# Rounded weight quarters transposed by VectorE in 32x32 squares and brought round through memory, instead of by TensorE

## What is computed

```
x = x + S4(x, lengths)            # long convolution over the 1024 positions, masked by a length
x = x + x W1^T + gated low rank   # top 2 of 8 experts, rank 16 each
x = x + x W2^T + low rank         # one of 5 labelers, rank 32
x = x + x w_eff^T                 # W3 rounded to a codebook, below
```

```
lora_delta = lora_B @ lora_A * (LORA_ALPHA / LORA_RANK)
normalized = (weight + lora_delta) / scale
idx = searchsorted(thresholds, normalized, side='left')
w_q = ((cb[idx] - normalized) + normalized) * scale
w_eff = w_q + lora_delta
```

## Time and profile before

| | us |
|---|---|
| three runs, median | 980.62 (980.40 to 981.99) |
| profiled execution | 980.34 |
| its span | 978.5 |
| TensorE busy | 968.8 (99%) |
| VectorE busy | 835.1 (85%) |
| ScalarE busy | 448.2 (46%) |
| GpSimd busy | 276.0 (28%) |
| DMA queue of SyncE, share of 16 engines | 44.2% |

### The profile page before, as it was taken

The page is one execution under the profiler, slowest core; times in us unless marked ns, Lnnn a source line. Parts: engine busy times, 40 slices in busy tenths (PEclk is TensorE's granted clock), DMA queues, the critical chain, the costliest instruction groups (busy, mean ns, idle before and its releaser), DMA issues.

```text
span 978.5 us, 16678 instructions
## 1 busy us (share of the span) xinstructions
PE 968.8 (99%) x4773; PEld 781.7 (80%) x4773; DVE 835.1 (85%) x1663; ACT 448.2 (46%) x855; POOL 276.0 (28%) x346
## 2 busy tenths in 40 slices
PE   9999999999999999999999999999999999999998
PEld 5455459888888788888888888888888888888886
DVE  6899999989954888888988888888889888888863
ACT  3342526253565445545445444455454455454541
POOL 6600100945434332222322223322223322223100
PEclk9999999999999999999999999999999999999999
DMA  8924010102133455555554545655556545555321
GB/s 283 124 46 86 0 44 1 44 1 44 29 68 64 76 109 93 100 98 99 115 103 89 109 90 106 112 95 98 101 96 115 105 87 104 96 104 112 76 44 44
DMA packets 380589, 83.46 MB, mean 85 GB/s; under 512 B 353144, under 2 KB 373432, under 8 KB 380552
## 3 DMA queue, kind: packets, MB, share of 16 engines
q1 hardware_dynamic: 379544, 82.28, 44.2%
q10 hardware_dynamic: 1008, 0.76, 0.3%
HBM read 60.89 MB, written 20.71 MB: 83 GB/s over the span
## 4 chain that ended last, share of the span: by engine, by line
PE 96%; ACT 1%; ACTq 1%; issue 1%; DVE 1%; POOL 0%; DVEq 0%; POOLq 0%
PE bank L816 35%; PE bank L1033 12%; PE bank L971 10%; PE bank L803 7%; PE bank L782 5%; PE bank L837 5%; PE bank L793 4%; PE bank L771 4%; PE bank L807 4%; PE bank L949 3%; PE bank L982 2%; PE bank L843 2%; PE bank L827 1%; PE bank L990 1%; PE bank L915 1%
## 5 line engine op out<-in xcount | busy, mean ns | idle before, releaser
L816 PE MATMUL bank<-Mh,strips_r 128*128 128x512 f32 x1020 | 289.1, 395 | 0.0
L816 PEld LDWEIGHTS bank<-Mh,strips_r 128*128 128x128 f32 x1020 | 189.9, 188 | 40.9
L1109 ACT ACTIVATE SK<-ZZ 64x448 f32<-64x448 f32 x128 | 73.9, 577 | 215.1 <-DVE ZZ L1463 212.7
L577 POOL TENSOR_TENSOR Cl<-QC,Ch 128x256 fp32r<-128x256 f32 x32 | 39.0, 1218 | 450.0 <-ACT Ch L1091 450.0
L816 PE MATMUL bank<-Ml,strips_r 128*128 128x512 f32 x510 | 160.0, 395 | 0.0
L1463 DVE SCALAR_TENSOR_TENSOR ZZ<-ZZ,coef 128x192 f32<-128x192 f32 (+1 forms) x256 | 106.6, 456 | 10.1 <-DVE ZZ L1454 0.2
L816 PEld LDWEIGHTS bank<-Ml,strips_r 128*128 128x128 f32 x510 | 95.9, 188 | 22.6
L971 PE MATMUL bank<-E,A 128*128 128x512 f32 (+1 forms) x320 | 97.8, 466 | 0.0
L1454 DVE SCALAR_TENSOR_TENSOR ZZ<-ZZ,coef 128x384 f32<-128x384 f32 (+1 forms) x128 | 80.0, 625 | 12.8 <-DVE ZZ L1463 6.7
L971 PEld LDWEIGHTS bank<-E,A 128*128 128x128 f32 x320 | 51.0, 191 | 44.9 <-issue 44.3
L803 PE MATMUL bank<-Mh,strips_r 128*128 128x296 f32 x256 | 70.7, 299 | 0.0
(11 more groups left out here) (319 smaller groups left out, 1840.3 us busy)
## 6 DMA issues: line engine op xcount, KB each, us to landing
X<-in_x SPq DMA_DIRECT2D x256, 64.0 KB, 2.3
XT<-in_x SPq DMA_DIRECT2D x256, 64.0 KB, 2.2
out_x<-O SPq DMA_DIRECT2D x62, 256.0 KB, 3.2
toep<-kpad SPq DMA_DIRECT2D x128, 64.0 KB, 2.2
E<-in_L_cond_W SPq DMA_DIRECT2D x8, 512.0 KB, 7.0
vq<-in_L_cond_weight SPq DMA_DIRECT2D x8, 512.0 KB, 3.4
turned<-TB SPq DMA_DIRECT2D x29, 128.0 KB, 2.0
Bt<-turned SPq DMA_DIRECT2D x116, 32.0 KB, 2.1
```

What stands on the lines that cost most here:

```text
L816: pe.matmul(psO[nh][:, :], xs[:, c, :], ms[:, c, nh * BANK:(nh + 1) * BANK], start=(c == 0 and n == 0), stop=False)
L1109: act.activation(SK[ri * N:(ri + 1) * N, hh, :].rearrange("p (c b) -> p c b", b=B), ZZ[hh * N:(hh + 1) * N, :, ri, :], ACT.Copy).then_inc( ...
```

## The change

TensorE's jobs a3, ScalarE's copies of them and GpSimd's diagonal sums go. When VectorE has rounded quarter q, it adds the identity to the two diagonal blocks, and transposes the quarter in squares of 32x32 into dq[q % 2], which is free by then. The SyncE queue writes dq to a new tensor `quarters` in memory so that the squares land in their turned places, and loads A3 from it in one DMA. New waits keep dq (ScalarE's next delta), the comparisons and the tables from overwriting what is not yet stored. Two waits of VectorE (v_ready, quant_init) move from ahead of the branches to behind them. On ScalarE and GpSimd `state_columns` and the first `expand_b` move from behind m(3, 0) to behind m(2, 9).

```diff
-        def stagings(q):
-            return [("a3", q, (q + k) % QUARTERS) for k in range(QUARTERS)]
...
         for mt in range(MT):
-            order += [("lap", mt)] + stagings(0)[mt:mt + 1]
+            order.append(("lap", mt))
...
+                def store_quarter(q):
+                    sp.wait_ge(q_turned, QT_TILES * (q + 1))
+                    for a in range(PARTS):
+                        dst = bass.AP(quarters.tensor, q * P * QCOLS + a * SPAN, [[QCOLS, SPAN], [P, QT_TILES * NC], [SPAN * QCOLS, PARTS], [1, SPAN]])
+                        sp.dma_start(dst, dq[q % 2][a * SPAN:(a + 1) * SPAN, :, :].rearrange("p t k -> p (t k)").rearrange(
+                            "p (n k j) -> p n k j", k=PARTS, j=SPAN)).then_inc(q_stored, 16)
+
+                def load_quarter(q):
+                    sp.wait_ge(q_stored, 16 * PARTS * (q + 1))
+                    sp.dma_start(A3[q % 2][:, :, :], quarters[q].rearrange("p (c o) -> p c o", c=NC)).then_inc(a3_loaded[q], 16)
...
                     elif name == "m":
...
-                            pool.wait_ge(a3_ready, QT_TILES * min(q + 2, QUARTERS))
...
-                        if j == ("m", LAST_Q, 0):
+                        if j == ("m", LAST_Q - 1, MT):
                             pool.wait_ge(cols_ready, 1)
                             expand_b(0, first=True)
...
-                        pe.wait_ge(stage_free, jobno[stagings(q)[-1]] + 1)
-                        pe.wait_ge(a3_ready, QT_TILES * (q + 1))
+                        pe.wait_ge(a3_loaded[q], 16)
...
                         if n == 0 and q >= 2:
                             act.wait_ge(quant_done, q - 1)
+                            act.wait_ge(q_stored, 16 * PARTS * (q - 1))
...
                         if 4 <= mt < 4 + FIXED:
+                            act.wait_ge(q_turned, QT_TILES)
                             compare(2, mt - 4)
...
-                        elif j == ("m", LAST_Q, 0):
+                        elif j == ("m", LAST_Q - 1, MT):
                             state_columns()
...
                     dve.tensor_tensor(vg, vg, inv_g, ALU.mult).then_inc(v_ready, 1)
...
-                    dve.wait_ge(v_ready, q + 1)
-                    dve.wait_ge(quant_init, q + 1)
...
                         with dve.If((n_kept & worth) > 0):
                             first = (n_kept >> (bit + 1)) << (bit + 1)
+                            dve.wait_ge(v_ready, q + 1)
+                            dve.wait_ge(quant_init, q + 1)
...
                     dve.tensor_tensor(qf, qf, df, ALU.add).then_inc(quant_done, 1)
+                    dve.wait_ge(quant_done, q + 1)
+                    for t in range(QT_TILES):
+                        d = qq[q][:, t, (q * QT_TILES + t) * P:(q * QT_TILES + t + 1) * P]
+                        step(dve.tensor_tensor(d, d, ident[:, :], ALU.add))
+                        dve.transpose(df.rearrange("p (c t k j) -> p t c k j", c=NC, k=PARTS, j=SPAN)[:, t],
+                                      qq[q][:, t, :].rearrange("p (c k r) -> p c k r", c=NC, k=PARTS)).then_inc(q_turned, 1)
...
-                dve.wait_ge(stage_full, jobno[stagings(1)[-1]] + 1)
+                dve.wait_ge(q_turned, QT_TILES * TURNED)
...
+                dve.wait_ge(q_stored, 16 * PARTS * TURNED)
                 angles(0)
```

More of the change, by code:

```diff
@@ L66, in resid_stack_kernel @@
     kpad = nc.dram_tensor("kpad", [H, 2, KP], F32, kind="Internal").ap()
+    QUARTERS = 4
+    TURNED = QUARTERS
+    quarters = nc.dram_tensor("quarters", [TURNED, P, 2 * L], F32, kind="Internal").ap()
     turned = nc.dram_tensor("turned", [P, HB * P], F32, kind="Internal").ap()
@@ L78, in place @@
         return t
-    QUARTERS = 4
     QO = L // QUARTERS
@@ L274, in resid_stack_kernel @@
         v_ready, above_done, w2_turned, nat_decay = sem("v_ready"), sem("above_done"), sem("w2_turned"), sem("nat_decay")
-        qt_full, qt_free, a3_ready = sem("qt_full"), sem("qt_free"), sem("a3_ready")
+        qt_full, qt_free = sem("qt_full"), sem("qt_free")
+        q_turned, q_stored, a3_loaded = sem("q_turned"), sem("q_stored"), [sem(f"a3_loaded{q}") for q in range(TURNED)]
         m_full, m_taken, m_lo, lowrank_hi, lowrank_lo = sem("m_full"), sem("m_taken"), sem("m_lo"), sem("lowrank_hi"), sem("lowrank_lo")
@@ L318, in resid_stack_kernel @@
                 order += [("m", q, mt)]
-                if q + 1 < QUARTERS and mt in (2, 4, 6, 7):
-                    order.append(stagings(q + 1)[(2, 4, 6, 7).index(mt)])
         jobs = [j for j in order if j[0] not in ("b3t", "qt0", "qt", "m")]
@@ L492, in _ @@
                 next_w2(7)
-                for q in range(2, QUARTERS):
-                    next_w3(q)
-                sp.wait_ge(stage_full, jobno[stagings(2)[-1]] + 1)
+                def store_quarter(q):
[7 more added lines that the diff above has]
+                    sp.dma_start(A3[q % 2][:, :, :], quarters[q].rearrange("p (c o) -> p c o", c=NC)).then_inc(a3_loaded[q], 16)
+                store_quarter(0)
+                next_w3(2)
+                store_quarter(1)
+                sp.wait_ge(quant_done, 2)
+                load_quarter(0)
+                sp.wait_ge(lowrank_lo, 3)
+                load_quarter(1)
+                next_w3(3)
+                store_quarter(2)
+                sp.wait_ge(m_full, mno["m", 0, MT] + 1)
+                load_quarter(2)
                 load_x(0, X, x_loaded)
                 load_x(0, XT, xt_loaded)
+                store_quarter(3)
+                sp.wait_ge(m_full, mno["m", 1, MT] + 1)
+                load_quarter(3)
                 for half in range(2):
@@ L697, in _ @@
                         pool.tensor_tensor(BLl[:, :], LAp[:, NC, :], BLh[:, :].bitcast(F32), ALU.subtract).then_inc(lowrank_lo, 1)
-                    elif name == "a3" and which[0] == which[1]:
-                        q = which[0]
-                        pool.wait_ge(stage_free, jobno[j] + 1)
-                        for t in range(QT_TILES):
-                            d = A3[q % 2][:, q * QT_TILES + t, t * P:(t + 1) * P]
-                            pool.tensor_tensor(d, d, ident[:, :], ALU.add).then_inc(a3_ready, 1)
                     elif name == "m":
@@ L984, in lap @@
                         start=(it == 0), stop=(it == NC - 1)))
-                def a3(q, n):
-                    if n == q:
-                        pe.wait_ge(quant_done, q + 1)
-                    several(("a3", q, n), 2 * QT_TILES, lambda ps, m: pe.transpose(
-                        ps[:, m * P:(m + 1) * P], qq[q][:, m % QT_TILES, (2 * n + m // QT_TILES) * P:(2 * n + m // QT_TILES + 1) * P], ident[:, :]))
                 def kern():
@@ L1034, in m @@
                     last.then_inc(m_full, 1)
-                do = dict(scale=scale_t, delta=delta, w2t=w2t, codesT=codes_t, codes=codes, nat4=nat4_t, wrt=wrt, qt0=qt0, qt=qt, lap=lap,
-                          a3=a3, m=m)
+                do = dict(scale=scale_t, delta=delta, w2t=w2t, codesT=codes_t, codes=codes, nat4=nat4_t, wrt=wrt, qt0=qt0, qt=qt, lap=lap, m=m)
                 for j in order:
@@ L1324, in _ @@
                             act.activation(BLh[:, :], LAp[:, NC, :], ACT.Copy).then_inc(lowrank_hi, 1)
-                    elif name == "a3":
-                        q, n = which
-                        if (q, n) == (0, 0):
-                            act.wait_ge(quant_done, 2)
-                        take(j, A3[q % 2][:, 2 * n:2 * n + 2, :], stage(j)[:, :].rearrange("p (t o) -> p t o", t=2))
                     else:
```

## The result

| us | before | after |
|---|---|---|
| median of the runs | 981.2 (980.40 to 981.99) | 994.99 (993.45 to 995.89) |
| ratio, 95% interval | | 1.0145 (1.0133 to 1.0157) |
| profiled execution | 980.34 | 995.89 |
| its span | 978.5 | 994.1 |

The changed kernel is slower by 1.45%: 13.8 us between the medians, 15.6 between the two profiled spans. The prediction was 990 in a range of 982 to 1001.

What follows compares the result with a forecast made beforehand. TensorE was taken as the bound before, the table chain after: angles 12.6 us late less 4.0 slack gives 8.6, plus 1.0 for the clock on 980.3 makes 989.9, called 990; range 982 to 1001.

Steps and rivals of the forecast that it cites:

- Bound and slack: Before the tiles: TensorE bounds the kernel; the table chain leading back to its state transpose has 4.0 us of slack.
- What goes from TensorE: Between laps and products m: 64 transposes in 16 groups go, 7.9 us, which become idle time and no gain.
- The laps' stall: TensorE before lap(0): 7.7 us idle until quarter 1 is stored, not on the path that ends last.
- The turn on VectorE: VectorE after rounding each quarter: two diagonal sums and two transposes cost 3.1 us, between 2.7 and 3.2.
- The moved waits: VectorE's rounding loop: branches run beside the product ahead of them, hiding the gaps; minus 6.4 us in all.
- The credit for GpSimd: VectorE's rounding: 1.5 us earlier because GpSimd's diagonal sums go; a choice between 0 and 3.
- The store: SyncE queue writing a quarter in 128-byte runs: 10 us from turned to stored, 8 at the low end, 18 high.
- Rival 1: Stores of quarters: slow small writes, stored after 18 us, giving 1005 us; chance 0.22 including results between.
- The SyncE queue: vq of quarter 3 behind the A3b load: tiles land about 193 and 194.5, wanted at 194.8, so just hidden.
- The clock: TensorE behind two idle stretches: slower transposes add 0 to 2 us on the path, taken as 1.
- Rival 2: Stores of quarters: nearly free at 4 us, so no change, 981.5 us; chance 0.10.
- Rival 3: TensorE stays the bound, so all 7.9 us of removed transposes are a gain: 972.5 us; chance 0.06.

Runs made afterwards that it cites:

- f0: The kernel before with only the waits on v_ready and quant_init moved behind the branches; 980.71 us, ratio 1.0003.
- e2: The changed kernel with all of delta(3, n) placed behind the nine laps in TensorE's and ScalarE's order; 993.05 us, ratio 1.0138.
- f5: The change for quarter 0 alone, the other three quarters turned by TensorE as in the kernel before; 979.48 us, ratio 0.9987.
- f1: The change for quarters 0 to 2, quarter 3 turned by TensorE as in the kernel before; 983.86 us, ratio 1.0030.
- e1: The changed kernel with the turned last quarter put into vq, so the angles need not wait for its store; 983.76 us, ratio 1.0039.
- e3: The changed kernel with 52 unread identity transposes filling TensorE's idle time before the state transpose; 995.86 us, ratio 1.0156.
- e4: The changed kernel with the waits on v_ready and quant_init put back ahead of the branches; 997.85 us, ratio 1.0169.
- g3: The kernel of e3 with 7 products of 128x512 columns in place of the 52 transposes; 992.39 us, ratio 1.0120.
- f3: The change for quarter 3 alone, quarters 0 to 2 turned by TensorE as in the kernel before; 987.30 us, ratio 1.0064.
- g1: The changed kernel with the edits of e1 and e2 together; 986.69 us, ratio 1.0064.

## Why the prediction was right, and where it was short

**Bound and slack: right.** The loss comes by the table chain. The exchanged tables land 16.9 us later (290.24 against 273.34) and the state transpose is 13.0 later; the difference is the 4.0 of slack, to a tenth. f0 shows from the other side that the table chain has time to spare. That TensorE stood for 5.60 us where about 6 were told is luck: it came to the state transpose at 289.8, not at 285, and QB was there at 295.4, not at 291. TensorE was 2.8 us later than told already at m(0, 0), 176.62 against 173.8, and then waited for Bw_parts for 2.90.

**What goes from TensorE, and that it is worth nothing: right.** No transposes, quarters of 32.7 us, and a time that is not shorter for it. e2 shows that TensorE's gains and stalls in the laps do not reach the end. The laps' stall was 7.93 (7.7 told), but at 154.40, 1.5 us later than told.

**The turn on VectorE: right.** 3.1 to 3.2 us a quarter (3.1 told), from f0, f5, f1, e1 and e3.

**The moved waits: mis-sized.** 6.4 told, about 4.1 to 4.4 measured (e4; f0, with its start taken off). I read "the branches run beside the product" from the 0.87 at quarter 1 and took the whole gap for hidden. A rest of 0.64 to 0.68 stays at three quarters of four. This is 2.0 to 2.3 us of the shortfall.

**The credit for GpSimd: wrong.** 1.5 told, as a choice. f0 to f5 leave none, and the change's own rows show why: GpSimd's long subtractions still fall on VectorE's sums. VectorE's timeline:

```profile
179.73 3.40 DVE L1823 TENSOR_TENSOR quant<-quant,vq 128x1024 f32<-128x1024 f32 x1
183.17 3.81 DVE L1824 TENSOR_TENSOR quant<-quant,vq 128x1024 f32<-128x1024 f32 x1
186.90 1.54 DVE L1823 TENSOR_TENSOR quant<-quant,vq 128x1024 f32<-128x1024 f32 x1
```

The sum of L1823 takes 3.40 us while GpSimd subtracts, until 187.35, and 1.54 behind that; L1824 takes 3.81 and then 1.63. In the kernel before GpSimd's subtractions fell on four instructions of VectorE ahead of these sums (L1813), which took 14.15 us; in the change the same four took 9.51. So VectorE lost 4 to 5 us in both kernels, in another place.

**The store: right.** 10 us told, 9.3 and 9.4 measured from the last transpose to the waiting instruction. Two rows of the table by stretches, the store of quarter 1 and the load of A3b, which comes in runs of 8 KB:

```profile
146.00:150.00 4.00, 0.46 (x3) 0.04 (x1) 3.33 (x3) 0.00 (x0) 0.00 (x0) 1.00 0.94 146
263.00:265.50 2.50, 2.50 (x13) 2.22 (x12) 2.40 (x4) 0.00 (x0) 0.00 (x0) 1.00 0.83 328
```

The store moves 146 GB/s at 0.94 of 16 engines, 13.2 ns for a run of 128 bytes, no more than the 13.7 of the reads in the earlier trace rows. Rival 1, dear small writes, has no support. Of the rule that the Trainium skill, "DMA: Bandwidth & Descriptors", Specifications, gives for transfers below 512 bytes, the trace agrees with one half: runs of 128 bytes are far from the rate of long ones, 146 against 328 GB/s. That a write below 512 bytes costs more than a read of that size is not seen. The 18 us were my doubling of the run time; the rule has no price.

**The SyncE queue: right.** The second half of quarter 3's weights was issued by 190.5 us, and VectorE took them at 198.96 without a wait.

**The clock: mis-sized.** 1 us told, between 0 and 2; 2.7 measured in the profiled execution (the code behind m(3, 3) is 15.6 late, the state transpose 13.0), 2.6 by g3. I took the price from short transposes and did not follow it to m(3, 3), whose 16 instructions run mostly at half clock as well: 6.02 us against 3.62.

**The sum again**, profiled execution against profiled execution. Told: angles 12.6 late, less 4.0, plus 1.0, is 9.6. Measured: the moved waits +2.1, GpSimd +1.5, the store -0.7, the start of the run +0.7 make the angles 16.2 late. Then +0.7 in the tables, -4.0, +2.7: 15.6. The start is no part of the change: VectorE's first step stands at 40.18 in this profiled execution and at 38.45 to 38.49 in e1 to e3, whose code is the same up to there, and the exponent product 1.4 us later than in e3; in the earlier trace rows the first step stands 0.7 us late in the same way. Of the 1.7 us, 0.8 is the product ahead of the first step, 3.11 us against 2.29; the GpSimd instruction beside it took 2.77 us instead of 5.34 (e3), so one of the two is held up. Why one execution starts later otherwise is open. It can account for some of the spread of the change's runs, 993.45 to 995.89.

**The rivals.** None came. Rival 2 (no change) needed a nearly free store; that came by another way in e1, which still lost 3.5 us: with four turns on VectorE the state transpose is 3.6 us late (286.02 against 282.44). Rival 3 (7.9 us faster) is nowhere near: the fastest of the kernels gains 1.0.

## What to carry to other kernels

Taking work from the busiest engine pays only up to the slack of the next chain, so before moving work, find what that chain must wait for, and give it the part that has time: here quarter 0, but not quarter 3. Count a buffer's release as part of the price: angles that overwrote the buffer being stored waited for 7.65 us, and another buffer took the loss from 1.45% to 0.39%. And price an idle stretch of TensorE with the half clock behind it, some 2 us here for stretches of 3 to 7 us.

## What the runs showed of the hardware

- Behind idle time of 3.23 (e4), 3.85 (f3), 5.60, 6.98 (g1) and 6.99 us (e2) TensorE's 16 instructions of m(3, 3) took 6.25, 6.18, 6.02, 5.66 and 5.40 us instead of 3.62; behind 1.04 (e1) and 1.00 us (g3, with work ahead) they took 3.62. The price did not grow with the stretch.
- TensorE can stand with no semaphore to wait for: 2.01 us in e3 and 0.55 in f5, both in the 128 products of about 10 ns each; none with fewer instructions ahead (g3). A DMA load of instructions stands 0.4 us ahead of the stop in e3 and 2.1 us ahead of it in f5; that TensorE waited for its instructions is the likely reading, not a shown one.
- Writes of 128-byte runs from the on-chip memory moved 146 GB/s, at 13.2 ns of one DMA engine a run; reads of such runs took 13.7 ns. Loads in runs of 8 KB moved 328 GB/s.
- A sum of 128x1024 on VectorE took 3.40 to 3.81 us beside GpSimd's subtractions of over 1,000 columns, 1.54 to 1.63 beside those of 256, and 1.18 in the earlier trace rows.
- The part behind the second state transpose, whose code is the same in all kernels, took 682.3 to 682.7 us in nine of the thirteen profiled executions (978.5 - 296.14 in the kernel before) and up to 684.7 in the others (986.1 - 301.44 in f3). A difference below some 2 us between two traces should be placed in the timeline before it is explained.
